# Keys and values as three single-pass products of rounded high and low parts, in a fused cross-attention and expert kernel

## What is computed

```python
q = (layernorm(x) @ Wq + bq).reshape(N, L, 16, -1)
k = (ctx @ Wk + bk).reshape(N, L, 16, -1)
v = (ctx @ Wv + bv).reshape(N, L, 16, -1)
qp = elu(q) + 1.0
kp = elu(k) + 1.0
# out_t = q_t . sum over s <= t of k_s v_s, divided by cumsum(qp)
x = x + (out / cumsum(qp)) @ Wo + bo

n = layernorm(x)
sel = argmax(softmax(relu(n @ W1 + b1) @ W2 + b2))
x = x + n @ expert_W[sel] + expert_b[sel]
```

## Time and profile before

| | |
|---|---|
| median of three timed runs | 1192.79 us |
| the profiled execution, its own time | 1187.42 us |
| span of that execution, first to last instruction | 1185.7 us |
| TensorE (PE) busy | 1053.6 us, 89% of the span |
| TensorE weight loads (PEld), beside PE | 734.8 us, 62% |
| VectorE (DVE) busy | 856.4 us, 72% |
| ScalarE (ACT) busy | 563.4 us, 48% |
| GpSimd (POOL) busy | 583.0 us, 49% |
| mean granted TensorE clock | 0.969 of full speed |

### The profile page before, as it was taken

One profiled execution on the slowest core, in us unless ns is written; L12 is line 12 of the kernel. 1 busy time (PEld: TensorE's weight loads), 2 busy tenths in 40 slices (PEclk: granted clock), 3 DMA queues, 4 the chain that ended last, 5 costly groups with the idle time before them and its releaser, 6 DMA issues. The chain is left out here.

```text
span 1185.7 us, 40628 instructions
## 1 busy us (share of the span) xinstructions
PE 1053.6 (89%) x15828; PEld 734.8 (62%) x15829; DVE 856.4 (72%) x1739; ACT 563.4 (48%) x945; POOL 583.0 (49%) x682
## 2 busy tenths in 40 slices
PE   2999999998989898989898989899999725999997
PEld 1666666666666666667676767666666614666664
DVE  2787887787878787878786878788887634555554
ACT  2545454544444454545444445444443113666654
POOL 4234444445454545444444445444453344777776
PEclk9999999999999999999999999999999857999999
DMA  3723333333333333333333333333322014666664
GB/s 102 236 74 91 92 92 92 94 95 95 90 96 94 100 89 102 99 90 98 92 109 90 98 94 108 94 91 93 91 74 73 20 45 130 191 191 185 190 183 135
DMA packets 88610, 127.44 MB, mean 107 GB/s; under 512 B 13693, under 2 KB 67584, under 8 KB 88320
## 3 DMA queue, kind: packets, MB, share of 16 engines
q1 hardware_dynamic: 75392, 89.98, 29.9%
q0 software_dynamic: 13056, 34.90, 7.8%
HBM read 73.03 MB, written 36.06 MB: 92 GB/s over the span
## 5 line engine op out<-in xcount | busy, mean ns | idle before, releaser
L586 DVE TENSOR_TENSOR stage<-b_s,causal 128x1024 f32<-128x1024 f32 x192 | 226.0, 1219 | 72.4 <-PE b_s L827 45.0
L466 POOL DMA_INDIRECT out<-stage x136 | 138.6, 1019 | 58.6 <-issue 31.0
L414 POOL DMA_INDIRECT buckets<-row,place x128 | 135.8, 1061 | 34.7 <-issue 34.7
L1019 PE MATMUL b_b<-we_sb,x3T 128*128 x544 | 150.5, 400 | 0.0
L813 PE MATMUL b_a<-xnT,wq_sb 128*128 128x512 f32 x256 | 128.4, 626 | 4.8 <-ACT xnT L506 2.2
L544 ACT ACTIVATE x3n<-stage 128x256 f32<-128x256 f32 x136 | 81.5, 599 | 90.4 <-DMA stage<-buckets 85.4
L813 PE MATMUL b_a<-ctxT,wk_sb 128*128 128x512 f32 x256 | 121.3, 618 | 1.8 <-ACT pos L485 1.8
L818 PE MATMUL b_b<-wo_sb,attT 128*128 128x256 f32 x512 | 118.4, 385 | 1.9 <-DVE attT L686 1.9
L818 PE MATMUL b_b<-wv_sb,ctxT 128*128 128x256 f32 x512 | 119.0, 386 | 0.0
L412 POOL TENSOR_TENSOR onehots<-onehots,onehot 128x32 bf16<-128x32 bf16 x32 | 7.8, 243 | 214.8 <-DVE place L619 214.8
L499 ACT ACTIVATE x2n<-row 128x256 f32<-128x256 f32 x128 | 66.5, 590 | 96.6 <-POOL row L430 96.6
(11 more groups left out here) (119 smaller groups left out, 1950.2 us busy)
## 6 DMA issues: line engine op xcount, KB each, us to landing
stage<-buckets SPq DMA_DIRECT2D x136, 130.0 KB, 2.3
x_in<-in_x SPq DMA_DIRECT2D x32, 512.0 KB, 4.8
ctxT<-in_ctx SPq DMA_DIRECT2D x32, 512.0 KB, 6.4
qsel<-qp SPq DMA_DIRECT2D x256, 64.0 KB
x_res<-in_x SPq DMA_DIRECT2D x32, 512.0 KB, 7.3
out<-stage POOLq DMA_INDIRECT x136, 2.7
we_sb<-in_L_ffn_expert_W SPq DMA_DIRECT2D x8, 256.0 KB, 5.8
buckets<-row,place POOLq DMA_INDIRECT x128
```

The costliest lines, as they stand in the source:

```text
L414: pool.indirect_dma_start(buckets, bass.IndirectOffsetOnAxis(place[:, slot(route), t:t + 1], 0), row[:, slot(route), t, :], None).then_inc ...
L466: pool.indirect_dma_start(out.rearrange("t p n -> (t p) n"), bass.IndirectOffsetOnAxis(rows2[:, r, TOKEN:TOKEN + 1].bitcast(U32), 0), sums ...
L586: dve.tensor_tensor(dst.rearrange("p g h s q -> p g (h s) q"), b_s[:, :, 256 * t:256 * t + 256].rearrange("p g (a q) -> p g a q", q=C), ca ...
L1019: last = pe.matmul(b_b[:, h, 0:D], x3T[:, h, P * k:P * k + P], we_sb[:, k, bass.ds(e, 1), :], start=(k == 0), stop=(k == KC - 1))
```

## The change

Weights `wk` and `wv` are loaded into the start of `stage`. ScalarE rounds each to a tile `_hi` of type `float32r`, and VectorE subtracts to get the rest, `_lo`. This is done once, at the start. For each group, in the stage `norm`, ScalarE rounds `ctxT` to `ctx_hi` and GpSimd subtracts to get `ctx_lo`; these two have one buffer each. Keys and values are then three products each, high by high, low by high and high by low, all of `float32r` operands, which are one sweep each over the array instead of the several of an fp32 product. The low by low product is left out. The other products stay in fp32.

```diff
-        wk_sb = sb("wk_sb", [P, KC, D])
-        wv_sb = sb("wv_sb", [P, KC, D])
+        wk_hi = sb("wk_hi", [P, KC, D], F32R)
+        wk_lo = sb("wk_lo", [P, KC, D], F32R)
+        wv_hi = sb("wv_hi", [P, KC, D], F32R)
+        wv_lo = sb("wv_lo", [P, KC, D], F32R)
...
+        ctx_hi = sb("ctx_hi", [P, KC, N], F32R)
+        ctx_lo = sb("ctx_lo", [P, KC, N], F32R)
...
@@ block.sync
                     if group_no(norm) >= 2:
-                        sp.wait_ge(s_v, n(norm, 2, -2))
+                        sp.wait_ge(s_clo, n(norm, k=-1))
                     sp.dma_start(ctxT[:, slot(norm), :, :], of_ctx(norm)).then_inc(s_ctx[slot(norm)], 16)
...
@@ block.gpsimd, step
+                if norm:
+                    pool.wait_ge(s_chi, n(norm, k=1))
+                    pool.tensor_tensor(ctx_lo[:, :, :], ctxT[:, slot(norm), :, :], ctx_hi[:, :, :].bitcast(F32),
+                                       ALU.subtract).then_inc(s_clo, 1)
                 if load:
                     pool.wait_ge(s_mv1, n(load, k=1))
...
@@ block.scalar
             act.wait_ge(s_wld, WEIGHTS)
+            act.activation(wk_hi[:, :, :], wk_in, ACT.Copy).then_inc(s_whi, 1)
+            act.activation(wv_hi[:, :, :], wv_in, ACT.Copy).then_inc(s_whi, 1)
...
+                if norm:
+                    act.wait_ge(s_ctx[slot(norm)], 16 * half(norm) + 16)
+                    if group_no(norm) >= 1:
+                        act.wait_ge(s_v, n(norm, 2))
+                    act.activation(ctx_hi[:, :, :], ctxT[:, slot(norm), :, :], ACT.Copy).then_inc(s_chi, 1)
                 if norm:
                     first_queries(norm, 0)
...
@@ block.vector
             dve.wait_ge(s_wld, WEIGHTS)
+            dve.wait_ge(s_whi, 2)
+            dve.tensor_tensor(wk_lo[:, :, :], wk_in, wk_hi[:, :, :].bitcast(F32), ALU.subtract).then_inc(s_wlo, 1)
+            dve.tensor_tensor(wv_lo[:, :, :], wv_in, wv_hi[:, :, :].bitcast(F32), ALU.subtract).then_inc(s_wlo, 1)
+            dve.wait_ge(s_wlo, 2)
...
@@ block.tensor
+            PARTS = ((0, 0), (1, 0), (0, 1))
+
+            def keys_of(dst, h):
+                w, c = (wk_hi, wk_lo), (ctx_hi, ctx_lo)
+                for k in range(KC):
+                    for i, j in PARTS:
+                        last = pe.matmul(dst, w[i][:, k, P * h:P * h + P], c[j][:, k, :],
+                                         start=(k == 0 and i == j), stop=(k == KC - 1 and j == 1))
+                return last
+
+            def values_of(dst, t):
+                w, c = (wv_hi, wv_lo), (ctx_hi, ctx_lo)
+                for k in range(KC):
+                    for i, j in PARTS:
+                        last = pe.matmul(dst, c[j][:, k, P * t:P * t + P], w[i][:, k, :],
+                                         start=(k == 0 and i == j), stop=(k == KC - 1 and j == 1))
+                return last
...
                 if project:
-                    a = slot(project)
-                    pe.wait_ge(s_ctx[a], 16 * half(project) + 16)
+                    if group_no(project) == 0:
+                        pe.wait_ge(s_wlo, 2)
+                    pe.wait_ge(s_clo, n(project, k=1))
                     pe.wait_ge(s_qe, n(project, 4, 4))
-                    channels_first(b_a[:, 0, :], wk_sb, ctxT[:, a, :, :], 0).then_inc(s_k, 1)
+                    keys_of(b_a[:, 0, :], 0).then_inc(s_k, 1)
...
-                        last = tokens_first(b_b[:, t // 2, D * (t % 2):D * (t % 2) + D], ctxT[:, a, :, :], wv_sb, t)
+                        last = values_of(b_b[:, t // 2, D * (t % 2):D * (t % 2) + D], t)
```

More of the change, by code:

```diff
@@ L5 @@
 F32 = mybir.dt.float32
+F32R = mybir.dt.float32r
 BF16 = mybir.dt.bfloat16
@@ L144, in build @@
         x3T = sb("x3T", [P, 2, D])
+        wk_in = stage[:, 0:KC * D].rearrange("p (k n) -> p k n", k=KC)
+        wv_in = stage[:, KC * D:2 * KC * D].rearrange("p (k n) -> p k n", k=KC)
         b_s = banks("b_s", RG)
@@ L175, in build @@
         s_v = sem("s_v")
+        s_whi = sem("s_whi")
+        s_wlo = sem("s_wlo")
+        s_chi = sem("s_chi")
+        s_clo = sem("s_clo")
         s_vs = sem("s_vs")
@@ L295, in load_weights @@
             def load_weights():
-                for dst, w in ((wq_sb, wq), (wk_sb, wk), (wv_sb, wv), (wo_sb, wo)):
+                for dst, w in ((wq_sb, wq), (wk_in, wk), (wv_in, wv), (wo_sb, wo)):
                     sp.dma_start(dst[:, :, :], w.rearrange("(k p) n -> p k n", p=P)).then_inc(s_wld, 16)
@@ L894, in step @@
                 if project:
-                    a = slot(project)
-                    pe.wait_ge(s_ctx[a], 16 * half(project) + 16)
+                    if group_no(project) == 0:
+                        pe.wait_ge(s_wlo, 2)
+                    pe.wait_ge(s_clo, n(project, k=1))
                     pe.wait_ge(s_qe, n(project, 4, 4))
-                    channels_first(b_a[:, 0, :], wk_sb, ctxT[:, a, :, :], 0).then_inc(s_k, 1)
+                    keys_of(b_a[:, 0, :], 0).then_inc(s_k, 1)
                     if route:
                         pe.wait_ge(s_place, n(route, k=1))
-                    channels_first(b_a[:, 1, :], wk_sb, ctxT[:, a, :, :], 1).then_inc(s_k, 1)
+                    keys_of(b_a[:, 1, :], 1).then_inc(s_k, 1)
                 elif route:
```

## The result

The changed kernel takes **1231.66 us** (median of 4 runs, 1229.4 to 1234.47) against 1193.7 us for the kernel before, timed beside it: a ratio of 1.0318, with a 95% interval of 1.028 to 1.0355. It is 3.2% slower. The forecast was 1200 us with a range of 1190 to 1216. The sign was right, and the time lies outside the range. The profiled execution has a span of 1232.0 us against 1185.7.

What follows compares the result with a forecast made beforehand. Odd steps were taken as bound by TensorE's list and the GpSimd-ScalarE chain to `xnT`. 0 (odd) + 0 (even) + 4.5 (start) + 3 (clock) = +7.5 us; profiled 1187.42 becomes 1195, median 1200 us, range 1190 to 1216.

Steps and rivals of the forecast that it cites:

- Even steps, 0 us: Even loop steps: `xnT` chain caps the gain, VectorE's `attT` is late next; 0, ends -7.4 and +3 us.
- Odd steps, 0 us: Odd loop steps: the 1.6 us saved go into waiting for `xnT` before the transposes of `x2n`; 0 for 16 steps.
- The price of the products, 2.72 and 2.88 us: TensorE's new key and value products per step, one sweep each, saving 0.91 and 0.68 us.
- rival 5: Key and value products: new ones no faster per sweep pair than old, 102 us more, 1295 us; chance 0.05.
- The start, +4.5: Kernel start: roundings and subtractions delay VectorE's first statistics and TensorE; +4.5 us, ends 2.6 and 8.
- The clock, +3: TensorE's clock: longer idles lower it in some odd steps, slack covers part in even ones; +3 us, ends -3.3 and +17.
- the fourth rival: Odd steps: clock falls in all of them, 21 us plus the start, 1214 to 1218 us; chance 0.13.
- VectorE, 0 with 2.14 us of slack: VectorE held up 2.37 us by GpSimd's `ctx_lo`, against 2.14 us idle before `attT`; taken as 0.
- Rival 6: GpSimd's hold on VectorE not covered: `attT` late by 1 us each step, 32 us, 1225 us; chance 0.05.
- The third rival: GpSimd's DMAs and small operations move up with TensorE: 1146 us at most, 1170 for half; chance 0.10.

Runs made afterwards that it cites:

- run 1: Changed kernel with 48 already fulfilled waits ahead of TensorE's first work, moving its loop 24 instructions further on: 1192.75 us, ratio 0.997.
- run 2: Kernel before with 192 already fulfilled waits, moving its loop 96 instructions to the changed kernel's place: 1238.58 us, ratio 1.0388.
- run 4: Changed kernel with 400 already fulfilled waits, moving its loop 200 instructions further on: 1236.8 us, ratio 1.0347.
- run 6: Kernel before with GpSimd's `z` times `u` first in each step and the indirect DMAs behind the small operations: 1181.24 us, ratio 0.9925.
- run 12: Kernel before with TensorE's loop written out and GpSimd's order changed to `z` first, DMAs later: 1135.07 us, ratio 0.9511.
- run 3: Changed kernel with its new work kept, but keys and values as plain fp32 products of the high parts: 1197.84 us, ratio 1.0041.
- run 9: Changed kernel with TensorE's loop written out, no jump, GpSimd's order as it was: 1173.19 us, ratio 0.9865.
- run 7: Changed kernel moved by 24 instructions, with GpSimd's `z` times `u` first and DMAs behind the small operations: 1173.04 us, ratio 0.9844.

## Why the prediction was wrong, point by point

- **Even steps, 0 us in the sum: the step that failed.** It took the twelve idles of the earlier trace rows as a price of the jump that the change leaves alone, and no rival had more of them. They are the time to fetch a block of instructions, and their number and length depend on where the loop lies in its list. The 96 instructions that the new products add ahead of the loop moved its start so that only four products fit between the jump's target and the end of its block: a second fetch, 2.5 us, and the lower clock in every even step. Measured: +3.58 us in each of 12, 43 us, where the sum had 0 with -7.4 and +3 us for all of them as ends. Runs 1, 2 and 4 show this cause from three sides.
- **Odd steps, 0 us: right.** 27.68 against 27.75 us. The saving of 1.24 us (I had 1.6) stands in the wait, which I put at 2.4 and which is 1.99. Runs 6 and 12 show that the wait hangs on GpSimd's chain: with its order changed, the wait for `xnT` is gone from both.
- **The price of the products, 2.72 and 2.88 us: right** within 0.3 us (3.00 and 2.95). It was one sweep, and rival 5 is out.
- **The start, +4.5: the delay was right, what is left of it too large.** The first statistics start at 15.14 us (in run 3 at 14.75), where I said 14.8, and TensorE's first transposes 2.9 us later than before (21.31 against 18.42). But the first logit products come only 1.1 us later (91.35 against 90.21), in run 3, which has the old products, 2.8. The step behind them is 1.7 us longer than before, at a granted clock of 0.94.
- **The clock, +3: wrong in place.** Odd steps never fell in the changed kernel, even ones always did. Where the second idle is taken away (run 1) 10 of 12 odd steps fall after their wait of 2 us and are 29.1 to 29.7 us long instead of 27.7: this is the fourth rival, in all but two steps. The stretches of such a step of run 1, its wait and then the transposes of `x2n` with the sums:

```profile
511.20:514.40 3.20, 1.21 (x66) 0.97 (x65) 3.07 (x6) 2.99 (x5) 2.57 (x3) 1.00 0.83 307
514.40:518.04 3.64, 3.64 (x72) 3.18 (x72) 3.60 (x3) 1.72 (x2) 3.33 (x1) 0.53 0.00 0
518.04:526.40 8.36, 8.36 (x209) 4.36 (x204) 4.89 (x10) 2.84 (x6) 6.25 (x6) 1.00 0.02 4
```

  The rule of the Trainium skill, TensorE: Matmul & The Clock Gate, Part 4, by which transposes do not count as busy for the clock in the same way, was set against this in the prediction. Run 1 fits it mostly, the odd steps of the changed kernel with the same wait and the same transposes do not. The waits ahead of these transposes in odd steps are 1.98 to 2.00 us long in both kernels, and the clock falls behind them in 10 of 12 steps of the one and in none of the other. In run 4, with the same waits, it falls in 9 of 12, although the even steps fall there too, and in run 9, with waits of 2.07 to 2.10 us in every step, in 6 of 25. So neither the rule nor the length of the wait decides alone, and what else does is open.
- **VectorE, 0 with 2.14 us of slack: right, with little left.** VectorE's idle ahead of `attT` fell from 47.3 us (48 records) to 20.9 (45), the running sum is now 4336 ns on average from 150 to 850 us, before 2292, while `u` went from 2043 to 1566:

```profile
L696 DVE TENSOR_TENSOR_SCAN z<-carry,qp 128x1024 f32<-128x1024 f32 x23 | 99.7, 4336 | 0.8
L713 DVE TENSOR_TENSOR attT<-b_b,u 128x512 f32<-128x512 f32 x45 | 29.0, 686 | 20.9 <-PE b_b L905 20.9
```

  TensorE did not wait for `attT`. Rival 6 came true only in run 7, when the steps had become shorter.
- **The third rival** (the chain is not fixed) needed an edit on GpSimd, and then gave 9 us even in the kernel before (run 6, 1190.64 beside it).

That run 1, without the loop's misplacement, comes near the sum (1192.75 us, forecast 1200) is partly luck. Its even steps are shorter (28.75 us against 30.13) by the jump's idle, 0.5 us shorter, by the clock, which falls in 2 of 12 and not in 5, and by some of the products' saving, and this pays for the odd steps in which the clock falls (29.21 against 27.75). The sum had 0 for both kinds of steps and +3 for the clock.

## What to carry to other kernels

An idle at the head of a loop that ends without a semaphore can be, as here, a fetch of instructions. Compare where the compiled loop starts and ends within its blocks before and after any change to the number of instructions, ahead of the loop too, and leave work between the jump's target and the end of its block: here 8 and 64 instructions were too few, 104 and 240 were enough. If a large change in time comes with unchanged work, move the loop by a few empty instructions before looking for a reason in the change itself. And before an operation is moved in a queue, list every chain that passes through the ones around it: the DMAs later with `z` first were worth 9 us in the kernel before, the DMAs later with `z` still behind them cost 135 in the moved kernel.

## What the runs showed of the hardware

- A jump back costs TensorE 1.7 to 2.9 us of idle here (means of 2.44 us in the kernel before, 2.10 in the changed one, 1.96 in run 1), and it fetches again although the same blocks ran one pass ago: 150 to 152 blocks in kernels whose loop touches nine blocks, 139 where it touches eight.
- The place of the loop's **end** counts as well. In the kernel before the loop ends 11 instructions into its ninth block. The records of the queue (us from the start of the ranks' first product to the fetch, and its length in ns; "restart" is the first score behind the jump) show two fetches that overlap ahead of its jump, and one in the moved kernel of run 1:

```
changed 548.87 restart 2.47  fetches: -0.63 (1313), +3.05 (931)
before  524.44 restart 3.00  fetches: -1.42 (876), -0.63 (1867), +3.70 (1369)
before  583.42 restart 2.95  fetches: -1.78 (1176), -0.58 (1678), +3.25 (1355)
run 1   530.90 restart 2.30  fetches: -0.71 (1128), +3.28 (876)
run 1   588.81 restart 2.64  fetches: -0.20 (876), +2.95 (1391)
```

  The first of the two seems to be the block behind the loop's end, which no one needs. The fetch 0.3 to 1.1 us behind the restart is, by theory A, that of the loop's next block. In the changed kernel it would be the one for which TensorE waits: in the first line it has landed at 3.98 us, and the fifth score starts at 5.48 (554.35 - 548.87), 1.5 us later.
- An operation of VectorE with two operands in SBUF did not merely wait for the GpSimd operation ahead of it: `u`, whose row begins at 363.84, 0.6 us before `x_res` of GpSimd, ended after `x_res` and the `ctx_lo` behind it. The Trainium skill, SBUF — State Buffer, section on the two separate sides, says that the one that starts first holds the ports until it ends. By the rows it was the other way round here. GpSimd's DMA issue from 363.45 to 364.41 alone does not explain it: in 14 of the 24 steps `u` begins 0.01 to 0.10 us after the start of the last DMA issue and takes 1.2 us, in five it begins 0.4 to 0.6 us after it and takes 6.2 to 6.4, and in the other five it begins 0.8 to 1.1 us after the start of `x_res` and takes 4.7 to 4.9. So it depends on how far GpSimd is when `u` begins; which of its instructions takes the ports, and when, no run here tells.
